# One string for a unit's order: the attention of a conditioned transformer block on one core

## The reference

```python
h = layernorm(x, g1, be1) * (1 + scale_msa) + shift_msa
q, k, v = h @ Wqkv + bqkv            # 16 heads of 32
attn = softmax(q @ k.T * 32 ** -0.5)  # per head, 1024 x 1024
h = (attn @ v) @ Wproj + bproj
x = x + gate_msa * h
h = layernorm(x, g2, be2) * (1 + scale_mlp) + shift_mlp
x = x + gate_mlp * (gelu(h @ W1 + b1) @ W2 + b2)   # 512 -> 2048 -> 512
x = rmsnorm(x) * (1 + scale) + shift  # scale, shift from the condition, quantised weights
```

## Time and profile before

| | |
|---|---|
| runs | 4074.07, 4077.33, 4079.95 us; median 4077.33 |
| the profiled execution | 4073.34 us, its span 4071.6 us |
| PE busy | 3995.4 us, 98% of the span |
| DVE, ACT, POOL busy | 2473.4, 1795.4, 1923.4 us |
| PE's clock | granted at 0.993 of full over the span |

### The profile page before, as it was taken

One profiled execution on the slowest core, in us unless ns is written; L12 is line 12 of the kernel. 1 busy time (PEld: TensorE's weight loads), 2 busy tenths in 40 slices (PEclk: granted clock), 3 DMA queues, 4 the chain that ended last, 5 costly groups with the idle time before them and its releaser, 6 DMA issues.

```text
span 4071.6 us, 51447 instructions
## 1 busy us (share of the span) xinstructions
PE 3995.4 (98%) x19723; PEld 2648.5 (65%) x19723; DVE 2473.4 (61%) x4020; ACT 1795.4 (44%) x3220; POOL 1923.4 (47%) x530
## 2 busy tenths in 40 slices
PE   8999999999999999999999999799999999999998
PEld 6778875445455455454455544588888888888886
DVE  3665557887777777777777775234445443344442
ACT  2222224665565555655555556333333333333332
POOL 1000005888788787887887878632211122231111
PEclk9999999999999999999999999999999999999999
DMA  5444463233323323323323330411110111201110
GB/s 199 175 173 176 183 210 102 53 73 76 75 64 82 78 53 84 76 55 84 74 65 74 74 78 26 142 55 42 34 42 34 42 39 50 62 34 42 34 42 21
DMA packets 184993, 323.70 MB, mean 80 GB/s; under 512 B 14452, under 2 KB 53428, under 8 KB 184748
## 3 DMA queue, kind: packets, MB, share of 16 engines
q1 hardware_dynamic: 184748, 320.41, 27.7%
HBM read 201.77 MB, written 117.54 MB: 78 GB/s over the span
## 4 chain that ended last, share of the span: by engine, by line
PE 94%; DVE 1%; DMA 1%; issue 1%; POOL 1%; ACT 1%; SPq 0%; POOLq 0%; ACTq 0%; DVEq 0%
PE psum L527 13%; PE psum L989 13%; PE psum L1002 12%; PE psum L428 10%; PE psum L430 9%; PE psum L429 9%; PE psum L1510 6%; PE psum L1514 6%; PE psum L1512 6%; PE psum L1018 4%; PE psum L1029 1%; PE psum L1031 1%; PE psum L1033 1%; PE psum L1472 1%; PE psum L463 1%
## 5 line engine op out<-in xcount | busy, mean ns | idle before, releaser
L817 DVE TENSOR_REDUCE max_part<-psum 128x1 f32<-128x512 f32 x2048 | 1298.6, 683 | 351.6 <-PE psum L527 340.8
L1121 ACT ACTIVATE probs<-psum 128x512 f32<-128x512 f32 x2048 | 1071.6, 599 | 686.1 <-PE psum L989 683.8
L1241 POOL TENSOR_TENSOR prob_sum<-prob_sum,probs 128x2048 f32<-128x2048 f32 x256 | 1175.8, 4593 | 111.7 <-ACT probs L1121 92.5
L1643 DVE TENSOR_TENSOR g_parts<-g_full,g_parts 128x512 fp32r<-128x512 f32 x256 | 311.7, 1217 | 776.0 <-ACT g_parts L1552 776.0
L527 PE MATMUL psum<-k_stack,q_stack 96*128 96x512 f32 x2048 | 758.2, 419 | 3.0 <-DVE max_part L817 1.3
L989 PE MATMUL psum<-q_stack,k_stack 98*128 98x512 f32 x2048 | 675.7, 411 | 4.9 <-DMA q_stack<-negmax_lo 2.5
L527 PEld LDWEIGHTS psum<-k_stack,q_stack 96*128 96x128 f32 x2048 | 387.5, 189 | 295.2 <-DVE max_part L817 235.9
L989 PEld LDWEIGHTS psum<-q_stack,k_stack 98*128 98x128 f32 x2048 | 372.1, 189 | 290.9 <-ACT probs L1121 250.2
L1548 ACT ACTIVATE g_full<-psum,cols 128x512 f32<-128x512 f32 x256 | 176.5, 690 | 823.4 <-PE psum L430 823.0
L1710 POOL TENSOR_TENSOR y_out<-y_out,rows 128x512 f32<-128x512 f32 x64 | 82.4, 1289 | 947.4 <-DVE y_out L1681 947.4
L1002 PE MATMUL psum<-probs,v_group 128*32 128x512 f32 x4096 | 517.4, 600 | 0.9 <-ACT probs L1121 0.9
(11 more groups left out here) (152 smaller groups left out, 4731.7 us busy)
## 6 DMA issues: line engine op xcount, KB each, us to landing
qk_parts<-qk_out SPq DMA_DIRECT2D x128, 512.0 KB, 2.8
k_stack<-qk_parts SPq DMA_DIRECT2D x96, 512.0 KB, 7.0
q_stack<-qk_parts SPq DMA_DIRECT2D x192, 256.0 KB, 9.4
x_in<-in_x SPq DMA_DIRECT2D x16, 1024.0 KB, 5.4
v_rows<-v_out SPq DMA_DIRECT2D x64, 256.0 KB, 2.0
v_group<-v_rows SPq DMA_DIRECT2D x32, 512.0 KB, 12.1
gated_attention<-gated SPq DMA_DIRECT2D x64, 256.0 KB, 4.6
x<-in_x SPq DMA_DIRECT2D x16, 1024.0 KB, 7.9
```

The lines of the kernel that those rows point to most:

```text
L817: dve.reduce_max(max_part[:, n:n + 1], psum[:, SMAX[at.turn % 3], :], AX.X).then_inc(dve_smax, 1)
L1121: act.activation(probs[slot(u, s)][:, h, j, :], psum[:, ST[k % 3], :], ACT.Exp, scale=SCALE).then_inc(act_exp, 1)
L1241: pool.tensor_tensor(prob_sum[u % 2][:, :, :], prob_sum[u % 2][:, :, :], probs[slot(u, s)][:, :, j, :], ALU.add).then_inc(pool_sum, 1)
```

## The change

The nested tuple becomes one string of a unit, read letter by letter by every engine. Letters: s, m and ! as before; V a group of values, D one of denominators, j one projection product (PE); g the gate, t, r, p, n turn, reciprocal, spread and normalise (DVE); w and a the copies of values and of the projection's input (ACT).

```diff
-    ORDER = (("mssm*mssm", "mssmm*mssmm"), ("mssm*mssm", "mssm*ssm"),
-             ("mssm*ssm", "mssm*ssm"), ("mssm*!mssm", "mssmm*mssm"))
-    LEAD = sum(x.count("m") for x in ORDER[-1])
+    ORDER = ("sgmsmsmsmDsmsmmssmasVDmssmsmmswDVtmrmmspssmVVV!n"
+             "VssmjmjmjjsjmsmssmjmjsmsjmjssmsmjsjmsmmjsssmmVV")
+    LAST = KT - 1
+    SUMMED = KT - 2
+    AHEAD = 0
+    LEAD = N_MAX + AHEAD - ORDER.split("!")[0].count("m")
+    PV_LAG = 2
+    RING = 6
...
-        probs = [s2(f"probs{i}", [P, GH, 2, CH]) for i in range(3)]
+        probs = [s2(f"probs{i}", [P, GH, CH]) for i in range(RING)]
...
-        def pe_score(pe, u, s, h, j):
+        def pe_score(pe, u, kt, h):
...
-        def pe_values(pe, u, s, j):
+        def pe_values(pe, u, kt):
...
-            if j == 0:
-                pe.wait_ge(act_exp, u * 32 + s * 8 + 8)
+            pe.wait_ge(act_exp, (u * KT + kt + 1) * GH)
...
+        def pe_project_product(pe, n, bank, m):
+            hi, lo = attn_hi[n % 2], attn_lo[n % 2]
+            if m == 0:
+                pe.wait_ge(act_ahi, n + 1)
+                pe.wait_ge(pool_alo, n + 1)
...
+                    elif what == "V":
+                        if values >= PV_LAG:
+                            pe_values(pe, u, values - PV_LAG)
+                        elif u:
+                            pe_values(pe, u - 1, values - PV_LAG + KT)
+                        values += 1
+                    elif what == "D" and u:
+                        pe_denominators(pe, u - 1, dens)
+                        dens += 1
+                    elif what == "j" and u - PROJ_LAG >= 0:
+                        if products == 0:
+                            pe.wait_ge(dve_attn, u)
+                        pe_project_product(pe, u - PROJ_LAG, DEN_BANK, products)
+                        products += 1
...
         def pe_tail(pe):
             at = TAIL[0]
-            pe_values(pe, NU - 1, LAST, 0)
-            pe_values(pe, NU - 1, LAST, 1)
-            pe.wait_ge(dve_gated, at)
+            for kt in range(KT - PV_LAG, KT):
+                pe_values(pe, NU - 1, kt)
+            pe.wait_ge(dve_smax, FIRST_TAIL)
+            pe_project(pe, at, tail_bank(at))
             pe_denominators(pe, NU - 1, 0)
             pe_denominators(pe, NU - 1, 1)
-            pe.wait_ge(dve_smax, FIRST_TAIL)
-            pe_project(pe, at, tail_bank(at))
+            pe_project(pe, at + 1, tail_bank(at + 1))
             pe_denominators(pe, NU - 1, 2)
-            for n, tile in enumerate(TAIL[1:], 1):
+            for n, tile in enumerate(TAIL[2:], 2):
```

More of the change, by code:

```diff
@@ L268, in piece_of, with slot, sums_done @@
             return (n + 1) * P > RAW
[L270 to L278, removed]
+        def slot(u, kt):
+            return (u * KT + kt) % RING
+        def sums_done(u, kt):
+            return (SUMMED - 1) * u + max(kt, 1)
         def sp_stage1(sp):
@@ L953, in sp_attention @@
                     load_gates(sp, b)
[L954 to L966, removed]
+                values = 0
+                for what in ORDER:
+                    if what == "!" and u + 1 < NU:
+                        send_max(sp, u + 1)
+                    elif what == "V":
+                        values += 1
+                        if values == PV_LAG and half == 0 and G + 1 < NGRP:
+                            if u:
+                                sp.wait_ge(pe_pv, KT * u)
+                            load_values(sp, G + 1)
+                    elif what == "g" and tile >= 1:
+                        store_gated(sp, tile - 1)
         def load_gates(sp, b):
@@ L1020, in pe_denominators @@
             i.then_inc(pe_den, 1)
-        def pe_project(pe, n, bank):
[L1023 to L1056, removed]
+        def pe_project_product(pe, n, bank, m):
[3 more added lines that the diff above has]
+                pe.wait_ge(pool_alo, n + 1)
+                if n == 0:
+                    pe.wait_ge(dve_wprojlo, 1)
+            k, kind = divmod(m, 3)
+            left, right = ((hi, wproj_hi), (hi, wproj_lo), (lo, wproj_hi))[kind]
+            i = pe.matmul(psum[:, bank, :], left[:, k, :], right[:, k, :], start=m == 0,
+                          stop=m == 3 * KD - 1)
+            if m == 3 * KD - 1:
+                i.then_inc(pe_proj2, 1)
+        def pe_project(pe, n, bank):
+            for m in range(3 * KD):
+                pe_project_product(pe, n, bank, m)
         def pe_attention(pe, at):
@@ L1104, in act_attention @@
                 tile = u - PROJ_LAG
[L1105 to L1129, removed]
@@ new lines, in act_attention @@
+                scores = 0
+                for what in ORDER:
+                    if what == "s":
+                        kt, h = divmod(scores, GH)
+                        k = u * KT + kt
+                        if h == 0 and k >= RING:
+                            pu, pk = divmod(k - RING, KT)
+                            act.wait_ge(pe_pv, k - RING + 1)
+                            if pk >= SUMMED:
+                                act.wait_ge(pe_den, 3 * pu + pk - SUMMED + 1)
+                            else:
+                                act.wait_ge(pool_sum, sums_done(pu, pk))
+                        n = k * GH + h
+                        act.wait_ge(pe_st, n + 1)
+                        act.activation(probs[slot(u, kt)][:, h, :], psum[:, ST[n % 3], :],
+                                       ACT.Exp, scale=SCALE).then_inc(act_exp, 1)
+                        scores += 1
+                    elif what == "w" and u:
+                        act_weigh(act, u - 1)
+                    elif what == "a" and tile >= 0:
+                        act_project(act, tile)
@@ L1380, in dve_tail @@
             dve.wait_ge(pe_den, 3 * NU)
-            dve.wait_ge(pool_sum, sums_done(NU - 1, 2))
-            for n, tile in enumerate(TAIL[1:], 1):
+            dve.wait_ge(pool_sum, sums_done(NU - 1, SUMMED - 1))
+            for n, tile in enumerate(TAIL[2:], 2):
                 dve_gate(dve, tile, tail_bank(tile))
```

111 lines of the change are left out of this document (49 added, 62 removed).

## The result

The kernel takes 4036.1 us (median of four runs, 4032.8 to 4038.4), against 4076.5 for the kernel before (median of four): a ratio of 0.990, with a 95% interval of 0.988 to 0.992. It is 40 us faster, where 64 were forecast: faster as expected, within the range, and 24 us short of the sum.

The account below looks back on a forecast made before the run. PE, without idle time in the repeating units, was taken to bound the kernel. Units 1.24 us shorter in 54 units give 67 us; with the tail's 4.8 back, 62 to 64 less: 4012 us, range 3988 to 4038.

Parts of the forecast that it names:

- term (2): Waits of scores and maxima for their banks in PE's units: all 0.91 us a unit goes; bounds 0.91 and 0.3.
- the account that closed at 30.08: Old unit on PE: 9.46 groups, 17.33 plain products, 2.38 for seven runs, 0.91 waits; 30.09 us measured.
- (1): Column-tile runs on PE: seven become six, as the transpose ends one; 0.34 us a unit gained, less 0.02.
- rival (A): The 16-column transpose stays in the column tiles: 0.34 us less in 63 units, 21 us, so 3991; chance 0.11.
- (3): Twelve projection products spread among scores and maxima stay at 0.228 us each: no change; bound 12 x 0.01.
- (4): Transpose nearer its maxima: DVE joins them in 4.9 us, PE needs 5.2, so not late, by 0.3 us.
- (5): Slots, POOL's sums and SP's loads in the units: no effect; bound for all 0.1 us a unit.
- (6): First nine units, without projection products: DVE's wait replaces the saving, 27.95 us stays; bounds 0 and -3 us in all.
- (8): Tail: denominators and a second projection now follow the wait for POOL, so SP's loads start 4.8 us later; bounds 0 and 5.5.

Follow-up runs that it names:

- before_short_max: The kernel before, with each maximum reduced over 64 of its 512 columns; 4043.1 us, units of 29.61 us.
- split_end: The kernel after, with a unit's last maximum moved between the last two value groups, one run more; 4056.1 us.
- turn_after_moved: The kernel after, with the transpose behind its fourth value group and the projection's first product seven plain products later; 4019.6 us.
- after_short_max: The kernel after, with each maximum reduced over 64 of its 512 columns; 4022.0 us, first nine units 26.96 us each.
- old_tail: The kernel after, with the tail of before: two last denominators ahead of the first projection, the third ahead of the second; 4030.1 us.
- searched: The kernel after, with an order found by the account (runs DD, VDV, VVVV, VV; transpose one product behind a run) and the old tail; 4005.5 us.
- down_by_bank: The kernel before, with the MLP's down products taken kind by kind over four banks, not bank by bank; 4077.8 against 4075.8 us.

## Why the prediction was right in its direction and 24 us off in its size

The step that failed is the size of term (2), and with it the account that closed at 30.08. I took the price of a plain product, 0.228, from the block of 12 and used it for the 64 scores and maxima too, which cost 0.234. What this left over I gave to waits, and counting places gave a like number, 7 x 0.05 + 4 x 0.14 = 0.91; that the two agreed to 0.01 us was luck. The places were counted rightly, and the prices were too high. The maxima waited 0.48 in all, not 0.56, as before_short_max shows. The scores cost 0.02 each and not 0.05: at seven places of the old unit a product behind a late score starts 0.25 us after it and not 0.234 (mean over 48 units), and the 0.49 us in the earlier trace rows from which I read 0.05 is 0.47 of ordinary pace and 0.02. So the waits were 0.62 us, not 0.91. With these prices the kernel before, without waits for DVE, is 9.46 + 64 x 0.234 + 12 x 0.229 + 7 x 0.34 + 7 x 0.02 = 29.70 us, and before_short_max measures 29.61; the kernel after is 9.46 + 76 x 0.234 + 6 x 0.34 + 0.02 = 29.30, and measures 29.23. Both are now 0.1 us high, so a step from one to the other is better than either. My forecast for the new unit was short by 0.4 us for the price of a plain product; in the old one, waits that were not there covered it.

Point by point:

(1) Runs: right. Six, not five; 0.32 to 0.34 us each, shown by split_end and turn_after_moved. The transpose breaks a run; rival (A), with the tiling by number of columns, is wrong by the 0.34 us in the timeline and the 0.33 of turn_after_moved. The rule on the drain of the Trainium skill, TensorEngine Tiling (Array Packing), "Key Properties", weighed there, agrees with this.

(2) Waits: all went, as said, but they were 0.62 us and not 0.91. It costs the forecast 54 x 0.29 = 16 us. (A score's bank comes round with the third score after it, as the step counts; the description of the kernel says the fourth.)

(3) Products one by one: they cost 0.234 each there, 0.227 to 0.229 in their block, so 12 x 0.006 = 0.07 us a unit, or 4 us in 54, within the bound of 0.12 and on its wrong side. With the waits this makes 0.36 of the missing 0.38 us a unit. They also are what spreads the maxima: the first nine units, which don't have them, still wait for DVE.

(4) and (5): right; nothing waits there. POOL has 5 us to spare in a unit.

(6) The first nine units: 28.10 for 27.95, so 1.3 us lost where I had none. That DVE bounds them is right (after_short_max); why they are 0.15 longer than before was not tried.

(8) The tail: the mechanism right and the size near, 5.3 us by the traces of old_tail and of the kernel after, beside 4.8. I had added durations from rows at full clock, and some 0.75 of the 5.3 come from the lower one. Against the kernel before there are 1.3 us more, since its trace is one in which the clock did not fall after the same idle time; which of the two comes is not forecast by anything here.

The parts, between the two profiled executions: 53 steps from one transpose to the next are 0.85 us shorter each, 45.1 us. The pieces of units ahead of the attention's first transpose and behind its last, up to the last two groups of values, give 0.3. The first nine units take 1.3 back, the stretch from the last groups to the load of x 6.6, and the time behind that load 1.3, for which no cause was sought. That is 36.2 us, beside 36.3 between the two spans. Forecast were 67 for the units, nothing for the first nine and 4.8 back in the tail, so the units make some 21 of what is missing; the medians say 40, since the profiled execution lay 3 us below the median before and 1 above it after.

## What to carry to other kernels

Price an instruction in the company it keeps: the same product was 3% dearer among others than in its block, and over 64 of them that was 0.38 us, where the waits one wanted to find were 0.62. An account that closes is no proof of its parts; shorten one engine's work, as in before_short_max, and the wait is measured by itself. And work that fits into a wait on the critical path costs nothing ahead of it, and its full length behind it: 5.3 us here.

## What the runs showed of the hardware that was not expected

Behind a run of column tiles, the next product starts 0.03 us after a transpose of 16 columns; within a run the transpose costs 0.34 us, and one product behind a run 0.11 (searched). A plain product's pace of 0.227 to 0.234 us is that of its weight load, 0.19 us and 0.04 behind it. After 3.34 and 3.38 us of the same wait for POOL, the clock was granted in full in the kernel before and fell in old_tail, and after 3.34 us it fell in down_by_bank: the same idle time came out either way. The price of 0.227 or 0.234 us for the same product depends on the stretch and on nothing that was tried.
